# Lambda convolution: the first image loaded in two halves, two constants made later, one read of averages moved

## The reference

```
keys    = softmax(xf @ Wk.T, axis=rows)
values  = batchnorm(xf @ Wv.T);  queries = batchnorm(xf @ Wq.T)
content_lambda   = einsum('bmk,bmv->bkv', keys, values)
position_lambdas = einsum('nmk,bmv->bnkv', E, values)
y = einsum('bknh,bkv->bhvn', queries, content_lambda)
  + einsum('bknh,bnkv->bhvn', queries, position_lambdas)
out = x + y
```

## Time and profile before

| | |
|---|---|
| median of 3 runs | 1439.04 us (1438.6 to 1439.9) |
| the profiled execution's own time | 1439.03 us |
| its span | 1437.3 us |
| PE busy | 1419.4 us, 99% |
| DVE busy | 827.2 us, 58% |
| ACT busy | 725.3 us, 50% |
| POOL busy | 432.6 us, 30% |

### The profile page before, as it was taken

The page is one execution under the profiler, slowest core; times in us unless marked ns, Lnnn a source line. Parts: engine busy times, 40 slices in busy tenths (PEclk is TensorE's granted clock), DMA queues, the critical chain, the costliest instruction groups (busy, mean ns, idle before and its releaser), DMA issues.

```text
span 1437.3 us, 37380 instructions
## 1 busy us (share of the span) xinstructions
PE 1419.4 (99%) x15048; PEld 1189.8 (83%) x15048; DVE 827.2 (58%) x1264; ACT 725.3 (50%) x1108; POOL 432.6 (30%) x366
## 2 busy tenths in 40 slices
PE   8998999999999999999999999999999999999998
PEld 8996888888888888888888888888888888888886
DVE  7988775555555555555555555555555555555553
ACT  6774465544554445444454455445444455445542
POOL 6682023232223322322223222322233222322230
PEclk9999999999999999999999999999999999999999
DMA  8833435353354434353354434443353434433441
GB/s 304 283 140 69 83 67 96 87 95 84 64 93 95 86 78 76 88 94 74 74 95 93 82 79 76 93 89 71 80 95 88 87 67 86 95 85 65 91 88 16
DMA packets 475814, 134.83 MB, mean 94 GB/s; under 512 B 339984, under 2 KB 471168, under 8 KB 475264
## 3 DMA queue, kind: packets, MB, share of 16 engines
q1 hardware_dynamic: 475776, 134.32, 43.5%
HBM read 109.12 MB, written 25.17 MB: 93 GB/s over the span
## 4 chain that ended last, share of the span: by engine, by line
PE 90%; DVE 1%; issue 0%; DVEq 0%
PE ps_a L1285 81%; PE ps_b L1297 5%; PE ps_a L1269 3%; DVE e_lo L775 0%; DVE first_b_lo L1036 0%; DVE first_b_lo L1038 0%; DVE lam_diag L953 0%; DVE pos L908 0%; DVE pos L916 0%; DVE res L942 0%; DVE inv_sum L948 0%; PE ps_b L1245 0%; DVEq L1035 0%
## 5 line engine op out<-in xcount | busy, mean ns | idle before, releaser
L1285 PE MATMUL ps_a<-v_hi,e_hi 128*128 128x512 f32 x1708 | 667.8, 391 | 0.0
L1285 PE MATMUL ps_a<-v_hi,e_lo 128*128 128x512 f32 x1708 | 664.6, 389 | 0.6 <-issue 0.6
L676 ACT ACTIVATE q_diag<-q_blk,q_shift_n,q_scale_n 128x256 f32<-128x256 f32 x512 | 409.7, 865 | 128.0 <-PE ps_b L1297 123.2
L595 ACT ACTIVATE e_hi<-e_nat 128x512 fp32r<-128x512 f32 x305 | 193.9, 636 | 479.6 <-PE ps_a L1285 197.2
L1285 PE MATMUL ps_a<-b_lo,e_hi 128*128 128x512 f32 x976 | 379.6, 389 | 0.0
L1285 PEld LDWEIGHTS ps_a<-v_hi,e_hi 128*128 128x128 f32 x1708 | 320.5, 188 | 66.9
L1285 PEld LDWEIGHTS ps_a<-v_hi,e_lo 128*128 128x128 f32 x1708 | 320.7, 188 | 65.4
L1285 PE MATMUL ps_a<-t_lo,e_hi 128*128 128x512 f32 x732 | 285.1, 389 | 0.0
L505 POOL TENSOR_TENSOR e_nat<-e_nat,s_buf 128x512 f32<-128x512 f32 x61 | 98.1, 1608 | 618.1 <-DVE e_lo L768 618.1
L768 DVE TENSOR_TENSOR e_lo<-e_nat,e_hi 128x512 fp32r<-128x512 f32 x305 | 222.0, 744 | 53.0 <-ACT e_hi L595 52.9
L1285 PEld LDWEIGHTS ps_a<-b_lo,e_hi 128*128 128x128 f32 x976 | 183.2, 188 | 38.2
(11 more groups left out here) (138 smaller groups left out, 985.8 us busy)
## 6 DMA issues: line engine op xcount, KB each, us to landing
e_nat<-in_L_conv_E SPq DMA_DIRECT2D x128, 512.0 KB, 3.8
res<-in_x SPq DMA_DIRECT2D x128, 128.0 KB, 4.3
out_dram<-res SPq DMA_DIRECT2D x124, 128.0 KB, 2.6
x_main<-in_x SPq DMA_DIRECT2D x24, 512.0 KB, 5.7
q_dram<-q_nat SPq DMA_DIRECT2D x4, 2048.0 KB, 8.2
q_blk<-q_dram SPq DMA_DIRECT2D x32, 256.0 KB, 3.3
x_more<-in_x SPq DMA_DIRECT2D x8, 512.0 KB, 9.2
out_dram<-res SPq DMA_DIRECT2D x4, 64.0 KB, 2.7
```

The source lines that it names most:

```text
L595: nc.scalar.activation(e_hi[:, i], e_source(i), ACT.Copy).then_inc(e_hi_ready, 1)
L676: ins = nc.scalar.activation(to[:, n], of, ACT.Identity, bias=q_shift_n[:, n:n + 1], scale=q_scale_n[:, n:n + 1])
L1285: ins = nc.tensor.matmul(BANK_OF[odd][i], e[:, i, j].rearrange("p n k -> p (n k)"), v[:, j], start=(STARTS[odd][i] and j == 0 and n == 0), ...
```

## The change

The first image's load becomes two loads of 512 columns each, with a semaphore each, and DVE waits for each half on its own. As the first load of slot 0 no longer counts on that slot's semaphore, the later waits for slot 0 are one load lower. The constants `fold` and `same_k` are made behind `gn_moments(6)`. `gn_finish(3)` is moved between the two halves of the first image of batch 4.

```diff
+        x_halves = [sem(f"x_halves{i}") for i in range(2)]
...
-            for i in range(GB // 2):
-                load_x(i, i)
+            for half in range(2):
+                part = slice(half * BANK, (half + 1) * BANK)
+                sp.dma_start(x_in(0)[:, part], x_v[:, 0, part]).then_inc(x_halves[half], 16)
+            load_x(1, 1)
             sp.dma_start(w_rows[0:QC, :], Wq).then_inc(weights_loaded, 16)
...
-            dve.wait_ge(consts, 6)
-            link(nc.vector.tensor_reduce(fold[:], ident[:].rearrange("p (m k) -> p k m", k=KD), AX.X, ALU.add))
-            nc.vector.tensor_copy(same_k[:].rearrange("p (m k) -> p m k", k=KD),
-                                  fold[:].unsqueeze(1).to_broadcast([P, TN, KD])).then_inc(same_k_ready, 1)
...
-                    dve.wait_ge(x_loaded[sl], 16 * (b // SLOTS + 1))
+                    if sl > 0:
+                        dve.wait_ge(x_loaded[sl], 16 * (b // SLOTS + 1))
+                    elif b > 0:
+                        dve.wait_ge(x_loaded[sl], 16 * (b // SLOTS))
                     for half in halves:
+                        if sl == 0 and b == 0:
+                            dve.wait_ge(x_halves[half], 16)
...
-            gn_moments(4, range(0, 1))
+            gn_moments(4, range(0, 1), range(0, 1))
             gn_finish(3)
+            gn_moments(4, range(0, 1), range(1, 2))
             gn_moments(4, range(1, 2))
...
             gn_moments(6)
+            dve.wait_ge(consts, 6)
+            link(nc.vector.tensor_reduce(fold[:], ident[:].rearrange("p (m k) -> p k m", k=KD), AX.X, ALU.add))
+            nc.vector.tensor_copy(same_k[:].rearrange("p (m k) -> p m k", k=KD),
+                                  fold[:].unsqueeze(1).to_broadcast([P, TN, KD])).then_inc(same_k_ready, 1)
             gn_moments(7, range(0, 2))
```

## The result

The changed kernel is slower: 1441.49 us (median of 22 executions, 1439.99 to 1446.17) against 1439.08 for the kernel before (22 executions, 1438.26 to 1441.89); ratio 1.0017, interval 1.0011 to 1.0023. That is 2.4 us, under the 0.2% that the prediction called a difference, but its interval is clear of no change. The prediction had 0.24 us the other way, and 1441.49 lies above its range (1437.5 to 1439.8). The profiled execution took 1441.02 (span 1439.3), 2.0 us more than the one of before. In all tables the ratio is to executions of the kernel before beside it on the same chip; the medians of the kernel before differ by up to 1.2 us between the sets (1438.96, 1439.35 and 1440.13), so times of different sets aren't compared.

What follows compares the result with a forecast made beforehand. TensorE's run of images was taken to bound the kernel, so only its earlier start counts: 0.24 us gained, 0 for the other terms, 1439.03 to 1438.79, predicted as 1438.8 us; range 1437.5 to 1439.8.

Steps and rivals of the forecast that it cites:

- What bounds the kernel: TensorE's gapless run of images: moving its start moves the end equally; other engines' work costs nothing until TensorE waits.
- The start at 9.95 as what sets the end: At the head, TensorE's first transpose of the first image, at 9.95 us, was taken to set the kernel's end.
- The first image in two halves: First image's load and statistics: halves land at 3.57 and about 4.20, sums ready at 5.33 instead of 5.98, 0.65 us sooner.
- (b): On TensorE, averaging could begin before the last warming matmul ends, about 5.80, at worst 5.98; read at 6.44 or 6.62.
- The added DMA issue: One more 0.45 us issue on SP at the head: landings taken as unchanged, cost 0, at most 0.45 us for the second image.
- Why 0.65 us do not arrive: The second image's half on DVE and TensorE's averaging behind the warming limit the first read's gain to 0.24 us.
- The constants: Two constants moved behind the sixth batch's statistics: 1.08 us into a 1.05 us DVE wait, 0.48 us cover left, cost 0.
- The moved read of the fourth batch: DVE's read of the fourth batch's averages between two statistics halves: cost and gain 0, unless TensorE is over 0.53 us earlier.
- Rival 1: TensorE's clock does not fall near 10 us, so the first image's projection comes 0.9 us sooner; 1437.9 us, chance 0.22.
- Theory C: From the experiments, not the prediction: the loss comes from TensorE's clock, falling at another place in each execution; no size given.
- Rival 3: Second image lands up to 0.45 us later, delaying the first read of averages: +0.14 to +0.6, 1439.2 to 1439.6; chance 0.15.

Runs made afterwards that it cites:

- halves_only: The kernel before with the first image loaded in two halves, with their waits, and nothing else; 1441.09 us, ratio 1.0016.
- more_warm: The kernel of whole_load with 8 and 13 warming matmuls where there were 4 and 7; 1441.42 us, ratio 1.0008.
- late_issue: The kernel before, with SP waiting for POOL's fourth constant between the issues of the first and second image; 1441.41 us, ratio 1.0013.
- half_on_act: The changed kernel with the first image's second half issued by ACT, so SP issues the second image at 1.27; 1439.39 us, ratio 1.0001.
- whole_load: The changed kernel with the first image in one load again, late constants and moved read kept; 1439.03 us, ratio 0.9998.
- reads_first: The changed kernel with the first two reads of averages ahead of the next image's statistics; 1441.57 us, ratio 1.0013.
- small_ahead: The kernel of whole_load with one 8 KB weight load issued between the first two images; 1440.67 us, ratio 1.0011.
- partition_halves: The changed kernel with each of the first image's two loads taking 64 partitions with whole 4 KB rows; 1440.20 us, ratio 1.0009.
- second_on_act: The changed kernel with the second image issued by ACT at 0.8 us on ACT's queue; 1441.56 us, ratio 1.0011.

## Why the prediction was wrong, point by point

- **What bounds the kernel**: right in that the run of images passes a delay on: from the second image's projection to 97 us the changed kernel kept its 1.84. Wrong where it lets nothing else move the end. From the first warming matmul behind the images to DVE's twenty-first instruction that turns `ps_a` into `pos`, near 218 us, the profiled executions need between 115.8 us (halves_only, changed) and 119.8 (more_warm), 116.7 before. That is why single executions do not follow their heads.
- **The start at 9.95 as what sets the end**: too narrow. The first image's transposes are only the first gate. The second image's transposes wait for ACT, which waits for the second read of averages, and in the changed kernel that read moved more (1.18) than the first (0.55).
- **The first image in two halves**: the first half at 3.57 was right (3.58), the second at 4.20 wrong (5.1, 5.1, 4.9 and 4.4 in four executions with the edit), the sums at 5.33 therefore too (6.24, and 5.58 in halves_only). The averaging can begin before the last warming matmul ends, as (b) had it: at 5.77 in halves_only.
- **The added DMA issue**: the step that failed. I took the landings as unchanged because bytes were already queued, and bounded the delay by the issue itself, 0.45 us. The second image landed 0.9 to 1.0 later, the third 1.9 (7.1 before, 9.0). late_issue shows the second image's delay without halves, half_on_act takes it away with them. A queue full of bytes was no cover for a later issue.
- **Why 0.65 us do not arrive**: the right places, the second image's landing and the averaging matmul, with the wrong landing in them. The read of the second average, behind the third image's half, I had put at 0.24 sooner, "since its data is there": it came at 9.65 against 8.47, 1.2 us later, and TensorE's second image follows it.
- **The constants**: right, whole_load. They take 0.36 + 0.23 us there rather than 1.08. POOL stands idle there, while the copy at 3.55 ran beside a fill of POOL's and took 0.67; that this is the reason is argued. (The forecast of 34.8 for their place did not follow from its own sum, which had them behind 37.49 - 0.24.) The read behind them (40.37, at 38.54 before) has 0.51 us of DVE idle before it left:

```profile
36.86 0.36 DVE L837 TENSOR_REDUCE fold<-ident 128x16 f32<-128x128 f32 x1
37.26 0.23 DVE L838 COPY same_k<-fold 128x128 f32<-128x128 f32 x1
...
40.37 0.21 DVE L753 TENSOR_REDUCE gn_out<-ps_b 128x12 f32<-128x48 f32 x1 [0.51 <-PE ps_b L1147]
```

- **The moved read of the fourth batch**: right, no cost and no gain in the median. In the head it may give 0.1 to 0.3 us: the second image's projection starts 2.54 us behind the first's in whole_load and more_warm, which have it, and 2.87 and 2.64 in halves_only and late_issue, which don't.
- **Rival 1, the clock**: its price in the head was right (0.9 to 1.0 us, whole_load and more_warm), but it didn't come with this change: the clock fell in the changed kernel too, 3 us later. It comes and goes between executions of kernels with nearly the same head (before, whole_load). That it is mere scatter is not shown (see Theory C). In the changed kernel the clock was at 0.50 from 14 to 15 us and again at 134 to 136, in rows of the same columns:

```profile
14.00:15.00 1.00, 1.00 (x6) 1.00 (x6) 0.93 (x5) 0.33 (x1) 0.89 (x2) 0.50 1.04 426
134.00:136.00 2.00, 2.00 (x6) 1.56 (x5) 1.78 (x6) 0.00 (x0) 0.00 (x0) 0.51 0.00 0
```

- **Rival 3, slower**: the mechanism that happened. Its place was right; its turning point (a landing at 5.95) no run tested, since all landings are below 5.8 or above 6.3. Its size was wrong: +0.14 to +0.6 where the kernel lost 2.4. I followed one read and stopped; the second read makes it about 1.3 at TensorE. The rest of the 2.4 no experiment assigns: a part comes with the lower clock, and waits of TensorE between 101 and 220 us move by more than that. I gave it 0.15. The Trainium skill (DMA: Bandwidth & Descriptors, section Bandwidth) has a rule that gives the right sign: it advises batches of at least 1 MiB, and cutting one transfer lost. Bandwidth was not what was lost, though: in half_on_act the engines moved 397 GB/s with the 256 KB halves, and the time was that of before. It was the issue more on SP.

Open: why a later issue lands later by twice as much. That the queue runs dry and the new transfer's first bytes are slow would fit the 140 GB/s at 3.6 us, but late_issue shows 369 there and still lands at 6.4, so it is argued and not shown. Over 3.6 to 4.8 us the engines move 389 to 410 GB/s in the three kernels that issue the second image at 1.27 (before, whole_load, half_on_act), 196 to 253 where SP issues it late with another transfer ahead, halves or not (both executions of the changed kernel, halves_only, reads_first, small_ahead, partition_halves), and 355 in late_issue. So a dip goes with each late issue, but its depth does not set the landing.

## What to carry to other kernels

At the head of a kernel the order and the hour of the DMA issues count, not only the bytes: an instruction more on the issuing engine ahead of the second transfer cost more than the first transfer's earlier half could give (ratio 1.0016 for halves_only, 1.0001 with the issue moved to another engine). When a load is cut in two, follow every later landing of that queue into each in-order stream that waits for it, and price all of them, not the first. A wait on data that stands ahead of a short read on the critical path makes that read as late as the data.

## What the runs showed of the hardware that was not expected

- The second transfer of the kernel landed about 0.2 us later for each 0.1 us that its issue was later (5.6 to 5.7 for 1.27, 6.4 to 6.6 for 1.74, 7.2 for 2.07); in late_issue the queue's bytes were the same as before.
- A transfer started from ACT's queue beside one from SP's slowed the other: the first half landed 3.3 us behind its issue with 256 KB beside it and 4.6 with 512 KB, against 2.6 to 2.8 with nothing on ACT's queue.
- DVE's `key_diag`, 128 x 128 elements, took 1.0 us in eight kernels and 2.2 in three (changed, second_on_act, half_on_act), the same instruction with POOL at work on two-operand instructions in both. In the profile of before it ends near the start of POOL's next instruction, 96.5; in the changed kernel it runs over the end of one, at 98.3, to the next, at 99.7. The Trainium skill (GPSIMD Engine Reference, section Key points) says that POOL shares its SBUF interfaces with VectorE and that they contend with VectorE's instructions in a 2-port mode or with two SBUF inputs. The ends in these traces would fit it; whether `key_diag` is such an instruction no run shows.
- TensorE waited 1.2 us in one execution (before), 2.0 in another (late_issue) and 3.0 in a third (more_warm), in the same stage, for nothing that the profile shows.
